# Moving a router into an attention loop: running ranks, scattered token numbers, expert weights split early

## The chip, the cores and the metric

The kernel runs on one core of a Trainium2 chip. The metric is the device time of one execution in microseconds (us). Engines are named as the profile names them: PE (matrix), PEld (its weight loads), DVE (vector), ACT (scalar), POOL (GpSimd), SP (the engine that issues most DMAs); "POOLq" or "SPq" is an engine's instruction queue.

## The reference

Two transformer layers on 16 x 256 tokens of width 256. Layer 0: layer norm, cross attention (16 heads of 16), residual; then a mixture of experts:

```
x = layernorm(x1)                                  # 4096 tokens
logits = x @ router_w + router_b                   # 16 experts
topv, topi = top_k(logits, 4); topw = softmax(topv)
gu = x @ gate_up[e] + bias;  act = (clip(up) + 1) * gate * sigmoid(1.702 * gate)
out = sum over the 4 chosen experts of topw * (act @ down[e] + down_bias[e])
```

Layer 1: layer norm and cross attention over batches at one position, residual, then a gated feed-forward with quantised weights, residual.

## The kernel before

Four parts run one after the other, each with an unrolled or looped schedule in which every engine has its own instruction list and semaphores order them. A part ends with a barrier, and `clear` (L44) sets an attention's semaphores to zero one by one on POOL.

**L0 attention** (`attention`, tag l0). 16 units of 256 tokens. `run_units` (L253) runs steps u = -5 to 16. In step u, with 16 sub-steps k (one a head), PE computes transposed scores of unit u (L554, into `ps_t`, two buffers), scores of unit u+2 (L567, into `ps_s`, two buffers) and the q, k, v projections of unit u+3; DVE takes the row maxima of `ps_s` (L453), ACT the exponentials of `ps_t` (L353). At k = 8 DVE makes the layer-norm statistics of unit u+4 (L439, L444), and POOL from them `rstd` (L331, L333), the normed tile `xn` (L337) and the residual with bias (L340); POOL also splits the context into high and low halves (L317, L319). DVE writes `v1` with its bias (L496) at k = 14, and the unit's output `yout` (L490) at k = 11 of the next step; SP stores it (L302). PE waits for the maximum of two slots before, and for the exponential of two slots before.

**Router** (`routed_experts`, first two blocks). Eight chunks of 512 tokens are loaded again from `x1`, normed, split into two f16 halves and stored as `moe_rows` (L762), transposed (L896) and multiplied with the router weights (L903); DVE adds the bias (L822), takes the eight largest (L827), their indices (L831). In the same loop the 16 experts' weights are loaded (L735, L736) and split: high half on ACT (L875, L876), low half on DVE (L857, L859). A second block computes on DVE ranks, first tiles and the row `pos` of each of the 16384 token-expert pairs (L944 to L978), and inverts that table into the token of each row by one-hot matmuls (L980 to L996, L1005, L1021). `slots` and `weights` go to memory in pieces of 16 bytes (L928, L929).

**Expert loop** (`cp_...`). 80 tiles of 256 rows. In step i POOL gathers the rows of tile i+3 with two indirect DMAs (L1109) by token numbers that DVE copied from SBUF (L1125); PE transposes tile i+1 (L1179), runs gate and up of tile i (24 matmuls, L1191) and down of tile i-2 (14 matmuls, L1200, L1202); DVE and ACT make the activation (L1131 to L1140, L1156, L1160), POOL its low half (L1114); ACT copies out y of tile i-2 (L1165) after `a_hi` of tile i, and SP stores it (L1091). All these orders are written out by hand.

**L1 attention** (L325 gathers eight times a unit what the experts wrote) and **gated_ffn** follow.

Of the kernel before, what the change touches and what calls it, by code (L numbers as in the profile page):

```python
# [7 lines left out]
ALU = mybir.AluOpType  # L8
# [9 lines left out]
P = 128  # L18
# [11 lines left out]
XB = 8  # L30
# [6 lines left out]
TILES = 80  # L37

# [24 lines left out]
def attention(nc, tag, x_in, x_out, ctx_t, w, masks, query_rows, key_rows, rows=None):  # L63
# [3 lines left out]
    with ExitStack() as ctx:  # L67
# [3 lines left out]
        adding = rows is not None  # L71
        K = 4
# [17 lines left out]
        w_raw = sb("w_raw", [P, 8, D])  # L90
# [6 lines left out]
        bv = sb("bv", [P, D])  # L97
# [3 lines left out]
        if masks:  # L101
            mraw = sb("mraw", [P, 2, QT, UNIT], I32)
# [15 lines left out]
        qs = sb("qs", [P, KQ, 8, UNIT], F16)  # L118
        ks = sb("ks", [P, KQ, H, UNIT], F16)
# [17 lines left out]
        yout = sb("yout", [P, 2, QT, D])  # L137

# [3 lines left out]
        w_high = sem("w_high")  # L142
# [3 lines left out]
        gp = sem("gp_setup")  # L146
        flagged = sem("flagged")
# [12 lines left out]
        with nc.Block() as block:  # L160
            @block.sync
            def _(sp):
# [9 lines left out]
                sp.dma_start(bv[:], w["bv"].partition_broadcast(P)).then_inc(const_loaded, 16)  # L172
# [6 lines left out]
                for i in range(2):  # L179
                    if masks:  # L180
                        sp.dma_start(mraw[:, i], masks[i]).then_inc(const_loaded, 16)
                sp.wait_ge(ks_set, 2)
                sp.dma_start(ks[96:rows_t].rearrange("p b h t -> p (b h t)"), key_rows).then_inc(rows_loaded, 16)
                if kinds:
                    sp.dma_start(qs[96:rows_s].rearrange("p b h t -> p (b h t)"), query_rows).then_inc(rows_loaded, 16)

# [7 lines left out]
            def _(pool):  # L194
                nc.gpsimd.memset(ident[:], 0.0).then_inc(gp, 1)
                nc.gpsimd.memset(ident16[:], 0.0).then_inc(gp, 1)
                nc.gpsimd.memset(half[:], -0.5).then_inc(gp, 1)
                pool.wait_ge(gp, 3)
# [4 lines left out]
                nc.gpsimd.memset(v1[:], 1.0).then_inc(gp, 1)  # L203

            @block.vector
            def _(dve):
                nc.vector.memset(ks[:, 0:2], 0.0).then_inc(ks_set, 1)
                for n, (src, dst, raw, by) in enumerate(weights):
                    dve.wait_ge(w_high, n + 1)
                    nc.vector.scalar_tensor_tensor(dst[:, 1], raw, by, dst[:, 0], ALU.mult, ALU.subtract)  # L210
                dve.wait_ge(const_loaded, 96 if masks else 64)
                dve.wait_ge(rows_loaded, 32 if kinds else 16)
                nc.vector.tensor_scalar(bq[:], bq[:], scale, None, ALU.mult)
                if masks:
# [10 lines left out]
                    nc.vector.tensor_copy(any_masked[:], count[:])  # L225

            @block.tensor
            def _(pe):
                if masks:
# [17 lines left out]
            "act": [xhi_done, qh_done, kh_done, mh_done, exp_done, osb_done, ahi_done],  # L247
            "dve": [stats_done, mv_done, xlo_done, ql_done, kl_done, v1_done, max_done, ml_done, rec_done, an_done, alo_done, y_done],
# [3 lines left out]

        def run_units(step):  # L253
            for u in range(-5, UNITS + 1):
                step(u)
# [386 lines left out]

# [958 lines left out]
```

## Time and profile before

| | |
|---|---|
| median of 3 runs | 1594.58 us (1590.15 to 1595.18) |
| profiled execution, its own time | 1595.34 us |
| its span, first to last instruction | 1593.5 us |
| granted TensorE clock, mean | 0.884 |
| busy: PE, DVE, POOL, ACT | 73%, 64%, 48%, 43% |
| L0 attention with its set-up, until its last store has landed | 0 to 421.5 us |
| router, until the first transposes of the expert loop | 421.5 to 600.9 us |
| expert loop | 600.9 to 996.2 us |
| L1 attention; feed-forward | 996.2 to 1410.7; 1410.7 to 1593.5 us |

A timeline row gives start, duration, engine, line, operation, output<-inputs, shape and count; the bracket is the engine's idle time before it and what ended it. For a DMA the duration is that of the issue, not of the transfer. In a table of windows each engine has its busy us and its instruction count.

### The profile page before, as it was taken

The numbers are of one execution on the slowest core, as the hardware profiler recorded it, in microseconds if no ns is written. First come the engines' busy times: TensorE is split into PE (matmuls) and PEld (weight loads), VectorE is DVE, ScalarE is ACT, GpSimd is POOL, SyncE is SP. The second block draws the span as 40 slices with busy tenths as digits, with TensorE's granted clock in tenths as the row PEclk, the third lists the DMA queues.
The fourth block names the chain that finished last, engine by engine and source line by source line (L and its number), as shares of the span: only waits on it lengthen the run. The fifth ranks groups of instructions, "written<-read, shape, count | busy, mean of one in ns | idle before, by whom it ended". The sixth has DMA issues, their size and how long they took to land. (4 is left out here: it accounts for less than half of the span.)

```text
span 1593.5 us, 35326 instructions
## 1 busy us (share of the span) xinstructions
PE 1168.3 (73%) x11045; PEld 890.5 (56%) x11047; DVE 1014.7 (64%) x2474; ACT 683.6 (43%) x1312; POOL 761.1 (48%) x783
## 2 busy tenths in 40 slices
PE   2688888888354248999999998026777777718997
PEld 1456666665153227888888887014666666504555
DVE  3777777775287995666666665137777776425563
ACT  1155555556253004555555554002444444524443
POOL 6332233310132376766666664488877772003443
PEclk9899999999755558999999999566999999958999
DMA  3212222210275412333333343544554452121231
GB/s 112 84 56 70 79 74 81 58 42 31 94 244 194 16 1 80 113 110 110 112 109 110 111 107 94 106 102 131 148 140 134 128 134 55 36 96 53 80 105 54
DMA packets 145101, 151.11 MB, mean 95 GB/s; under 512 B 32024, under 2 KB 131144, under 8 KB 144968
## 3 DMA queue, kind: packets, MB, share of 16 engines
q1 hardware_dynamic: 131168, 111.94, 24.3%
q0 software_dynamic: 13824, 37.77, 9.1%
q8 instruction: 63, 1.03, 0.3%
q14 instruction: 46, 0.38, 0.1%
HBM read 86.06 MB, written 37.88 MB: 78 GB/s over the span
## 5 line engine op out<-in xcount | busy, mean ns | idle before, releaser
L353 ACT ACTIVATE l_pt<-l_ps_t 128x512 f32<-128x512 f32 (+1 forms) x512 | 244.2, 493 | 296.7 <-PE l_ps_t L554 290.3
L453 DVE TENSOR_REDUCE l_mx<-l_ps_s 128x2 f32<-128x512 f32 (+1 forms) x512 | 274.3, 547 | 135.7 <-PE l_ps_s L567 135.3
L1191 PE MATMUL cp_ps_g<-cp_xt,ex_gu_hi 128*128 128x256 f16 x1280 | 216.6, 275 | 7.2 <-issue 4.4
L567 PE MATMUL l_ps_s<-l_ks,l_qs 96*128 96x256 f16 (+1 forms) x1024 | 172.3, 255 | 55.3 <-issue 35.7
L1109 POOL DMA_INDIRECT cp_rows<-moe_rows,cp_slot_token x160 | 169.1, 1057 | 45.0 <-issue 26.7
L1191 PE MATMUL cp_ps_g<-cp_xt,ex_gu_lo 128*128 128x256 f16 x640 | 175.6, 274 | 0.0
L554 PE MATMUL l_ps_t<-l_qs,l_ks 100*128 100x256 f16 (+1 forms) x1024 | 166.1, 248 | 4.6 <-ACT l_pt L353 3.9
L325 POOL DMA_INDIRECT l_picked<-expert_rows,l_slots x128 | 130.9, 1023 | 57.6 <-issue 37.0
L1131 DVE TENSOR_SCALAR cp_gate<-cp_ps_g,ex_g_bias 128x256 f32<-128x256 f32 x160 | 70.1, 479 | 123.1 <-PE cp_ps_g L1191 123.1
L1114 POOL TENSOR_TENSOR cp_a_lo<-cp_act_f,cp_a_hi 128x512 f16<-128x512 f32 x80 | 92.5, 1156 | 93.4 <-ACT cp_a_hi L1160 93.4
L1191 PEld LDWEIGHTS cp_ps_g<-cp_xt,ex_gu_hi 128*128 x1280 | 120.8, 98 | 26.7 <-issue 12.3
L567 PEld LDWEIGHTS l_ps_s<-l_ks,l_qs 96*128 96x128 f16 (+1 forms) x1024 | 89.0, 100 | 78.9 <-issue 51.4
L1151 ACT COPY cp_xt<-cp_ps_x 128x1024 f16<-128x1024 f16 x80 | 80.3, 1003 | 75.9 <-PE cp_ps_x L1179 75.9
L331 POOL TENSOR_SCALAR l_rstd<-l_mv 128x2 f32<-128x2 f32 x32 | 7.6, 238 | 217.5 <-DVE l_mv L444 217.3
L554 PEld LDWEIGHTS l_ps_t<-l_qs,l_ks 100*128 100x128 f16 (+1 forms) x1024 | 92.6, 99 | 31.2 <-ACT l_pt L353 13.9
L1160 ACT CAST cp_a_hi<-cp_act_f 128x512 f16<-128x512 f32 x80 | 49.4, 618 | 132.0 <-DVE cp_act_f L1140 132.0
L1376 POOL TENSOR_TENSOR ff_hlo<-ff_hf,ff_hhi 128x512 f16<-128x512 f32 x48 | 55.7, 1167 | 85.1 <-ACT ff_hhi L1405 85.1
L1202 PE MATMUL cp_ps_y<-ex_dn_hi,cp_a_hi 128*128 x320 | 87.5, 274 | 0.0
L1202 PE MATMUL cp_ps_y<-ex_dn_hi,cp_a_lo 128*128 x320 | 87.5, 273 | 0.0
L1202 PE MATMUL cp_ps_y<-ex_dn_lo,cp_a_hi 128*128 x320 | 87.5, 273 | 0.0
L337 POOL TENSOR_SCALAR l_xn<-l_xin,l_mv,l_rstd 128x256 f32<-128x256 f32 x64 | 77.8, 1223 | 3.4
L576 PE MATMUL l_ps_b<-l_ident,l_xn 128*128 128x128 f32 x128 | 22.6, 305 | 67.8 <-POOL l_xn L337 67.8
(228 smaller groups left out, 2912.4 us busy)
## 6 DMA issues: line engine op xcount, KB each, us to landing
expert_rows<-cp_yout SPq DMA_DIRECT2D x80, 256.0 KB
l_qs<-l_nat SPq DMA_DIRECT2D x96, 128.0 KB
l_ks<-l_nat SPq DMA_DIRECT2D x192, 64.0 KB, 2.6
l_cin<-in_ctxT SPq DMA_DIRECT2D x32, 256.0 KB, 2.9
x<-l_yout SPq DMA_DIRECT2D x64, 128.0 KB, 1.8
rt_raw<-in_gate_up SPq DMA_DIRECT2D x16, 512.0 KB, 4.3
l_xin<-in_x SPq DMA_DIRECT2D x32, 128.0 KB, 2.2
rt_xin<-x SPq DMA_DIRECT2D x8, 512.0 KB, 4.4
```

The costliest lines, as they stand in the source:

```text
L325: nc.gpsimd.indirect_dma_start(picked[:, n % 2, q, k], None, y_rows, bass.IndirectOffsetOnAxis(ap=slots[:, n * QT + q, k:k + 1], axis=0)). ...
L337: nc.gpsimd.tensor_scalar(xn[:, q], xin[:, n % XB, q], mv[:, q, 0:1], rstd[:, q:q + 1], ALU.subtract, ALU.mult).then_inc(xn_done, 1)
L353: nc.scalar.activation(pt[:, h % 8], ps_t[:, h % 2, :, 0:span], ACT.Exp).then_inc(exp_done, 1)
L453: nc.vector.reduce_max(mx[:, n % 2, :, 8 * (k % 2) + k // 2], ps_s[:, k % 2, :, 0:span], AX_X).then_inc(max_done, 1)
L554: last = nc.tensor.matmul(ps_t[:, h % 2, kt, 0:span], ks[0:rows_t, u % KQ, key_head, kt * P:kt * P + P], qs[0:rows_t, u % KQ, h // 2, seen ...
L567: last = nc.tensor.matmul(ps_s[:, h % 2, q, 0:span], qs[0:rows_s, n % KQ, h // 2, q * P:q * P + P], ks[0:rows_s, n % KQ, key_head, seen], ...
L1109: nc.gpsimd.indirect_dma_start(rows[:, n, h], None, rows_dram[:, :], bass.IndirectOffsetOnAxis(ap=slot_token[:, n, h:h + 1], axis=0)).then ...
L1114: nc.gpsimd.tensor_tensor(a_lo[:, b], act_f[:, b], a_hi[:, b], ALU.subtract).then_inc(alo_done, 1)
L1131: nc.vector.tensor_scalar(gate[:, b, m], ps_g[:, b, m], g_bias[:, bass.ds(e, 1), m], LIMIT * WS, ALU.add, ALU.min).then_inc(gate_done, 1)
L1151: nc.scalar.copy(xt[:, 1 - b], ps_x[:, 1 - b]).then_inc(xt_copied, 1)
L1191: last = nc.tensor.matmul(ps_g[:, b, m], wt[:, bass.ds(e, 1), c, m * P:m * P + P].rearrange("p o n -> p (o n)"), xt[:, b, part, c], start= ...
L1202: last = nc.tensor.matmul(ps_y[:, b, h], a[:, b, c, h * P:h * P + P], wt[:, bass.ds(e, 1), c].rearrange("p o n -> p (o n)"), start=False, ...
```

## The change

- `attention` for layer 0 gets a `route` object. The router's work is done there by units: in step u unit u-2's output is normed again (statistics from `yout` at k = 12 and 14 of the step before; four small POOL operations; two ACT activations at k = 3), split in halves (ACT at k = 5, POOL), stored, transposed by PE into a `ps_t` slot (k = 6), multiplied with the router weights into a `ps_s` slot (k = 12); DVE makes logits, maxima, indices and one-hot. In step u unit u-3 gets its ranks (PE, a `ps_s` slot at k = 4, against counts so far), positions (DVE), and POOL scatters its token numbers with eight indirect DMAs into `route.table`, a memory table with a fixed stretch of 4096 rows for each expert. The loop has two more steps (u = 17, 18).
- Expert weights 0 to 7 are loaded and split in steps -5 to 0 (`EXPERTS_AT`), 8 to 15 inside the first 16 tiles of the expert loop (`late_expert`), because `qs` and `ks` of the attention share SBUF with them. Weights of wq to wo and the mask are loaded into the experts' raw buffers. XB is 7 in layer 0.
- `v1` is written by ACT without bias; the bias goes through `wo` into `bo` in the set-up, in both layers.
- The router's two blocks are replaced by one short block (counts to tiles, first table row of each tile, weights, bias rows).
- In the expert loop the token numbers of a tile come by a DMA of SP from `route.table` at a row read from a register, instead of by a DVE copy; slots are computed in four DVE pieces in steps 1, 3, 5, 7 and stored by SP in step 9. The expert part ends with a `clear`.

The diff, cut to what the prediction speaks of:

```diff
@@ attention
+        XB = 7 if routing else 8
+                if routing:
+                    sp.dma_start(rw[:], route.rw); sp.dma_start(rb[:], ...)
+                    sp.wait_ge(zeroed, 1)
+                    sp.dma_start(route.table..., pt[...][:, 0:ROWS // P]).then_inc(table_set, 16)
                 sp.wait_ge(ks_set, 2)
                 sp.dma_start(ks[96:rows_t]..., key_rows)
+                dve.wait_ge(bv_done, 1)
+                nc.vector.scalar_tensor_tensor(bo[:], ps_b[:, 0], 1.0 / WS, bo[:], ALU.mult, ALU.add)
+        EXPERTS_AT = {-5: (0,), -4: (1, 2), -3: (3, 4), -2: (5,), -1: (6,), 0: (7,)} if routing else {}
+        ITERATIONS = range(-5, UNITS + (3 if routing else 1))
@@ sync, step u
+                def load_expert(e):
+                    if e >= 2:
+                        sp.wait_ge(e_low, 2 * (e - 1))
+                    route.load_expert(sp, e, e_loaded[e % 2])
+                    n = u - 2
+                        sp.dma_start(route.rows(n), xh[:, n % 2]...).then_inc(rows_stored[n % 2], 16)
+                    for e in EXPERTS_AT.get(u + 1, ()):
+                        load_expert(e)
+                    sp.wait_ge(scattered, 16 * QTILES * TOP)      # after the loop
@@ gpsimd, step u, in this order
+                    n = u - 2
+                        pool.wait_ge(mv2_done, c1 + 2 * n + 2)
+                        nc.gpsimd.tensor_scalar(rstd2[:], mv2[:, :, 1], EPS, None, ALU.add).then_inc(var2_done, 1)
+                        nc.gpsimd.tensor_scalar(shift2[:], mv2[:, :, 0], -1.0, None, ALU.mult).then_inc(minus_done, 1)
+                        nc.gpsimd.tensor_tensor(rstd2[:], rstd2[:], half[:], ALU.pow).then_inc(rstd2_done, 1)
+                        nc.gpsimd.tensor_tensor(shift2[:], shift2[:], rstd2[:], ALU.mult).then_inc(shift2_done, 1)
...
+                        pool.wait_ge(xhi2_done, c1 + n + 1)
+                        nc.gpsimd.tensor_tensor(xh[:, n % 2, :, 1], xn2[:], xh[:, n % 2, :, 0], ALU.subtract)
...
+                    n = u - 3
+                        pool.wait_ge(pos_done, c1 + n + 1)
+                        for q in range(QT):
+                            for k in range(TOP):
+                                nc.gpsimd.indirect_dma_start(route.table, bass.IndirectOffsetOnAxis(ap=route.pos[:, t, k:k + 1], axis=0),
+                                                             token_id[:, t:t + 1], None).then_inc(scattered, 16)
@@ scalar
+                    def norm_again(n):                            # k == 3, n = u - 2
+                        act.wait_ge(shift2_done, c1 + n + 1)
+                        for q in range(QT):
+                            nc.scalar.activation(xn2[:, q], yout[:, n % 2, q], ACT.Identity, bias=shift2[:, q:q + 1], scale=rstd2[:, q:q + 1])
+                    for e in EXPERTS_AT.get(u, ()):               # end of step u; DVE likewise with expert_low
+                        expert_high(e)
@@ routed_experts, first block
+                for e in (EARLY, EARLY + 1):
+                    route.load_expert(sp, e, e_loaded[e % 2])
+                sp.wait_ge(rows_zero, 1)
+                sp.wait_ge(bias_split, 2)
...
+                sp.wait_ge(weighed, 1)
+                sp.dma_start(weights_dram.rearrange("(t p) k -> p t k", p=P), wts[:]).then_inc(tables_stored, 16)
+                sp.wait_ge(bias_set, 32)
@@ expert loop, sync, step i
+                        if live(i, 3):
+                            if live(i, 1):
+                                sp.wait_ge(gathered[n], at_gather(i + 1, n))
+                            row = first_of(i + 3)
+                            sp.dma_start(row_token[:, n], route.table[bass.ds(row, R), :]...).then_inc(idx_loaded[n], 16)
                         if live(i, -2):
                             sp.wait_ge(y_copied, at(i - 2))
-                            sp.dma_start(y_dram[...].rearrange("(q p) d -> p q d", p=P), yout[:, b])
+                            sp.dma_start(y_dram[...].rearrange("(p h) d -> p h d", h=2), yout[:, b])
+                        if isinstance(i, int) and i == 9:
+                            sp.wait_ge(slot_step, 5)
+                            sp.dma_start(slots_dram..., slot[:]).then_inc(tables_stored, 16)
+                        e = late_expert(i)                        # 8 + i // 2 for even i < 16
+                        if e is not None and e + 2 < E:
+                            sp.wait_ge(e_low, 2 * (e - EARLY) + 2)
+                            route.load_expert(sp, e + 2, e_loaded[e % 2])
@@ gpsimd, step i
-                            pool.wait_ge(idx_set, at(i + 3))
+                            pool.wait_ge(idx_loaded[n], (i + 3 - n) * 8 + 16)
@@ vector and scalar, end of step i
+                            act.wait_ge(e_loaded[e % 2], 32 * ((e - EARLY) // 2 + 1))
+                            for part, raw in zip((0, 2), route.raw_parts(e)):
+                                nc.scalar.activation(route.part(e, part), raw, ACT.Copy, scale=WS).then_inc(e_high, 1)
+                            dve.wait_ge(e_high, 2 * (e - EARLY) + 2)
+                            for part, raw in zip((1, 3), route.raw_parts(e)):
+                                nc.vector.scalar_tensor_tensor(route.part(e, part), raw, WS, route.part(e, part - 1), ALU.mult, ALU.subtract)
@@ tensor, before gate and up of tile i
+                            if isinstance(i, int) and EARLY <= i < E:
+                                pe.wait_ge(e_low, 2 * (i - EARLY) + 2)
@@ class Route
+    def load_expert(self, sp, e, loaded):
+        sp.dma_start(self.raw[:, e % 2, 0:KC], self.gate_up[e * D:e * D + D, :]...).then_inc(loaded, 16)
+        sp.dma_start(self.raw[:, e % 2, KC]..., self.down[e * D:e * D + D, :]...).then_inc(loaded, 16)
```

## Rows read from the trace of the kernel before

**Rows 1.** Windows: router, expert loop; busy us (x instructions) by engine, clock, DMA.

```profile
421.50:600.88 179.38, 67.26 (x321) 53.43 (x323) 143.69 (x479) 40.69 (x50) 78.11 (x110) 0.50 0.47 120
600.88:996.20 395.32, 380.34 (x3680) 332.05 (x3680) 250.32 (x558) 213.22 (x321) 258.20 (x237) 0.98 0.35 106
```

**Rows 2.** Waits of SP at the end of L0: total us, times, longest.

```profile
SPq L46 <- PEq L46: 4.2, 1, 4.2
SPq L306 <- DMA x<-l_yout: 3.1, 1, 3.1
```

**Rows 3.** Windows: one unit of the L0 loop in its steady part.

```profile
222.03:243.93 21.90, 19.44 (x196) 13.86 (x195) 16.51 (x35) 12.51 (x25) 6.42 (x8) 1.00 0.24 74
```

**Rows 4.** Timeline of POOL: rstd of units 0, 5 and 15 in L0.

```profile
22.00 0.23 POOL L331 TENSOR_SCALAR l_rstd<-l_mv 128x2 f32<-128x2 f32 x1
...
111.75 0.23 POOL L331 TENSOR_SCALAR l_rstd<-l_mv 128x2 f32<-128x2 f32 x1 [14.63 <-DVE l_mv L444]
...
332.67 0.23 POOL L331 TENSOR_SCALAR l_rstd<-l_mv 128x2 f32<-128x2 f32 x1 [13.27 <-DVE l_mv L444]
```

**Rows 5.** Groups of the router stage: count, busy us, mean ns, idle before.

```profile
L903 PE MATMUL rt_ps_l<-rt_rw,rt_xt 128*128 128x16 f32 x128 | 28.7, 375 | 9.3 <-ACT rt_xt L882 9.3
...
L875 ACT ACTIVATE ex_gu_hi<-rt_raw 128x1024 f32 x12 | 12.6, 1054 | 5.4 <-DMA rt_raw<-in_down 5.4
L876 ACT ACTIVATE ex_dn_hi<-rt_raw 128x512 f32 x12 | 7.4, 618 | 0.0
...
L857 DVE SCALAR_TENSOR_TENSOR ex_gu_lo<-rt_raw,ex_gu_hi 128x1024 f32 x12 | 14.5, 1210 | 0.0
L859 DVE SCALAR_TENSOR_TENSOR ex_dn_lo<-rt_raw,ex_dn_hi 128x512 f32 x12 | 8.1, 677 | 0.0
```

**Rows 6.** Timeline of DVE across a step's end in L0.

```profile
229.75 0.74 DVE L496 SCALAR_TENSOR_TENSOR l_v<-l_ps_b,l_bv 128x256 f32<-128x256 f32 x2
...
233.51 0.69 DVE L453 TENSOR_REDUCE l_mx<-l_ps_s 128x2 f32<-128x512 f32 x1 [0.18 <-PE l_ps_s L567]
```

**Rows 7.** Timeline of POOL: residual after xn; an indirect gather in L1.

```profile
225.69 1.26 POOL L340 TENSOR_TENSOR l_xin<-l_xin,l_bo 128x512 f32<-128x512 f32 x1
...
1185.12 0.95 POOL L325 DMA_INDIRECT l_picked<-expert_rows,l_slots  x1 [0.30 <-issue]
```

**Rows 8.** DMA issues: count, KB each, median us to landing.

```profile
rt_raw<-in_gate_up SPq DMA_DIRECT2D x16, 512.0 KB, 4.3
rt_raw<-in_down SPq DMA_DIRECT2D x16, 256.0 KB, 5.3
slots<-ex_pos SPq DMA_DIRECT2D x1, 64.0 KB, 12.1
weights<-ex_wts SPq DMA_DIRECT2D x1, 64.0 KB, 19.0
rt_rw<-in_router_w SPq DMA_DIRECT2D x1, 16.0 KB, 1.8
```

**Rows 9.** Timeline of one tile of the expert loop.

```profile
640.52 0.59 ACT L1165 ACTIVATE cp_yout<-cp_ps_y 128x512 f32<-128x512 f32 x1
...
641.18 0.27 PE L1200 MATMUL cp_ps_y<-ex_bias_rows,ex_two_rows 128*128 x1
641.35 14.47 SPq L1091 DMA_DIRECT2D expert_rows<-cp_yout  x4
...
642.08 0.97 POOL L1109 DMA_INDIRECT cp_rows<-moe_rows,cp_slot_token  x1
...
647.47 0.61 PE L1179 MATMUL cp_ps_x<-ex_ident,cp_rows 128*128 128x128 f16 x8
```

**Rows 10.** Waits in 640 to 980 us.

```profile
PEld cp_ps_x L1179 <- DMA cp_rows<-moe_rows,cp_slot_token: 2.2, 6, 0.4
```

**Rows 11.** Timeline: a DVE copy beside a POOL operation in the router.

```profile
472.07 2.12 POOL L799 TENSOR_TENSOR rt_xh<-rt_xn,rt_xh 128x1024 f16<-128x1024 f32 x1 [2.57 <-ACT rt_xh L880]
...
472.36 1.87 DVE L832 COPY rt_best<-rt_high 128x16 f32 x1
```

More of the change, by code:

```diff
@@ new lines, in step @@
+                        if routing and k == 4 and live(n):
+                            at = s_at["rank", n]
+                            pe.wait_ge(max_done, c1 + at - 1)
+                            pe.wait_ge(took_done, c1 + n + 1)
+                            for q in range(QT):
+                                earlier = [(route.ones[:], took[:, n % 2, a]) for a in range(1 + q)] + [(before[:], took[:, n % 2, 1 + q])]
+                                for i, (l, r) in enumerate(earlier):
+                                    last = nc.tensor.matmul(ps_s[:, at % 2, 0, q * E:q * E + E], l, r, start=i == 0, stop=i == len(earlier) - 1)
+                            last.then_inc(s_done, 1)
@@ new lines, in step @@
+                        n = u - 2
+                        if routing and k == 12 and live(n):
+                            at = s_at["logits", n]
+                            pe.wait_ge(max_done, c1 + at - 1)
+                            pe.wait_ge(exp_done, c1 + t_at["turn", n] + 1)
+                            for q in range(QT):
+                                for c in range(KC):
+                                    last = nc.tensor.matmul(ps_s[:, at % 2, 0, q * E:q * E + E], xt2[:, c, q * P:q * P + P], rw[:, c], start=c == 0, stop=c == KC - 1)
+                            last.then_inc(s_done, 1)
@@ new lines, in routed_experts @@
+        fills = sb("fills", [P, E]); one_e = sb("one_e", [P, E]); tile_id = sb("tile_id", [P, 1]); tile_row = sb("tile_row", [P, 1])
+        over = sb("over", [P, E, E]); tiles = sb("tiles", [P, E]); end = sb("end", [P, E]); jump = sb("jump", [P, E])
+        past = sb("past", [P, E - 1]); jumped = sb("jumped", [P, E - 1]); owner = sb("owner", [P, 1]); base = sb("base", [P, 1])
+        expert = sb("expert", [1, TILES], U32); first_row = sb("first_row", [1, TILES], U32)
+        region = sb("region", [P, E - 1]); posf = sb("posf", [P, T * K]); slot = sb("slot", [P, T, K], U32)
@@ L1081, in expert_of, with first_of, late_expert @@
                 return nc.values_load(expert[0:1, bass.ds(i, 1)], engines=[engine], min_val=0, max_val=E - 1,
-                                      skip_runtime_bounds_check_because="the minimum with E - 1 bounds it")
+                                      skip_runtime_bounds_check_because="it counts ends of 15 experts")
+            def first_of(i):
+                return nc.values_load(first_row[0:1, bass.ds(i, 1)], engines=[mybir.EngineType.SP], min_val=0, max_val=ROWS - R,
+                                      skip_runtime_bounds_check_because="a tile past an expert's end is of the next expert, and the last region holds every tile")
+            def late_expert(i):
+                return EARLY + i // 2 if isinstance(i, int) and i % 2 == 0 and 0 <= i // 2 < LATE else None
             with nc.Block() as block:
```

808 lines of the change are left out of this document (427 added, 381 removed).

## The prediction

> **What bounds the kernel now.** I read first the table of windows by stage [rows 1]. From the last landing of L0 [rows 2] to the first transposes of the expert loop there are 179.4 us in which PE works 67 at half clock and DVE 144: the stage that the change removes. In the expert loop PE is busy 380 of 395 us: that stage is PE's, unless something starves it. Then one unit of L0 [rows 3]: 21.9 us, PE busy 19.4, DVE 16.5, ACT 12.5, POOL only 6.4. PE bounds it, with DVE close by, and POOL is nearly free. The steps follow each other at (332.67 - 111.75) / 10 = 22.1 us [rows 4]. Last the waits and the timeline of the expert loop [rows 9, 10]: PE waits on gathered rows 6 times in 340 us, 2.2 us in all. So the gathers arrive just in time. The change makes the gathers later, and this is why the loop needs a working of its own.
>
> **The removed stage.** After: barrier and clear as before, 4.2 + 0.6 us for 58 semaphores [rows 2]; the 32 more at the same rate add 2.5. Then the short block. The DVE chain with two PE transposes is some 25 small operations, about 8 us; POOL's bias-row memset ends at about 6 us. SP sends the bias rows at 7 and the softmax weights at 9.5. The block does not wait for the latter, but they are 4096 pieces of 16 bytes; the like table took 12.1 us to land, and its twin behind it on the queue 19.0 [rows 8]. The first token-number load sits behind them on SP's queue, and lands at 21.8 us instead of 16. Two gathers (2.8 us) and their landing (1.9) follow: 26.5 us after the block's start. 4.8 + 2.5 + 26.5 = 33.8; gain 179.4 - 33.8 = **-145.6** (-138 to -151: the table stored slower, or not in the way).
>
> **L0, set-up: +3** (+1 to +4). Three more DMAs (0.4 us of issue each) and a table of zeros ahead of the key rows, whose landing opens DVE's last stretch; `bo` gets one more operation. L1's set-up gets the latter.
>
> **L0, filling: +16** (+8 to +20). Expert 0 is loaded in about 5 us [rows 8], split by ACT in 1.05 + 0.62 and by DVE in 1.21 + 0.68 [rows 5]. All that stands ahead of unit 0's statistics on DVE, which end at 22 us now [rows 4] and then at about 32.6: 10 us beyond the set-up's. Expert 2 can be loaded only when expert 0 is split, so ACT and DVE reach unit 0's transposed tile at 38 and 40: no more lost, as `xn` comes then too. Experts 3 and 4 end 2.5 us after the first scores, 5, 6 and 7 cost about 1.2 each at a step's end, since `v1` leaves DVE.
>
> **L0, steady steps: +33** (+22 to +50). Per unit PE gets 4 transposes (0.6 us, as L604 has them), the logits: 28.7 us for 4096 tokens at half clock [rows 5], so 0.9 a unit at full clock, and 5 small rank products (0.4): 1.9. DVE gets 3.4 us (two statistics 0.74, the rest fifteen operations of 0.07 to 0.3) less 0.74 for `v1`. Part of it falls at k = 12 to 0, where DVE has no gap now [rows 6]; at k = 4 to 7 it has some. That makes 25 us a step. POOL has a chain of its own. After the statistics at k = 8 it makes `xn` and the residual, 4.9 us (222.0 to 226.95 [rows 3, 7]); then eight scatters. No scatter is in the trace; the nearest row is a gather of 128 rows, 0.95 + 0.30 [rows 7], so 10.3 with the slower ones. I take it, since the instruction makes 128 descriptors either way; half (small elements) and double are the ends. Then the four small operations for the next norm, 1.8, on which ACT waits at k = 3 before further exponentials, and PE behind it at k = 6; from there to the statistics it is 8.2. Sum 25.2. Both chains are about equal: 25.4. Steps 3 to 11 (those with scatter and statistics): 9 x 3.3 = 30; step 2: 3. With scatters at half the step is PE's 24.5, +22 in all. Steps 12 to 15: **+10** (+6 to +14), 2.5 each, PE's 1.9 and a hop.
>
> **L0, tail: +29** (+20 to +38). The last unit now ends with a store that lands 3.8 us after `yout`. After: statistics, four POOL operations, norm, halves: POOL is free at about 8 us for the scatters of unit 14 (10.3), then of unit 15 (10.3), landing 1.9: 30.4. So +26.6, and 2 for the work between.
>
> **The skill, beside the trace.** A DVE copy of 16 columns took 1.87 us beside a POOL operation that ended at the same moment [rows 11]. The Trainium skill (SBUF — State Buffer, SBUF: two separate sides) says that a VectorE operation with two SBUF inputs, or in a two-port mode, and a GpSimd operation lock each other out of a shared port for the whole instruction; the trace agrees. By that rule the added one-hot and rank product would lose up to 1 us a step beside POOL's 15 us of work; the sum would be about 10 us higher. I have not added it.
>
> **Expert loop, tiles 18 to 79: +27** (+5 to +60). Call T the end of gate and up of tile i. One tile before the rows shown T is 636.5 (641.2 less a period of 4.7). `yout` of tile i-2 ends at 641.1 [rows 9], T + 4.6, and its store is issued at T + 4.85. Before, the gather of tile i+4 starts at 642.08, T + 5.6, and PE takes its rows at 647.47, T + 11, with some 0.9 us to spare. After, SP issues the token-number load only behind that store: T + 5.4, plus a register read that the trace doesn't show (0.1 to 1; I take 0.3, as SP's other waits cost little). The smallest landing is 1.8 [rows 8], but it follows a store of 256 KB: 2.2. So the gather starts at T + 7.9, 2.3 later; less the spare 0.9, 1.4 us late over three tiles, 0.46 a tile, x 59 = 27. If the load lands at 1.6 the loss is 15; if 4 us, +60. POOL's `a_lo` behind the gather is still in time.
>
> **Tiles 0 to 17: +38** (+20 to +55). In even steps to 10 SP waits, after the store, until DVE has split an expert. ACT starts its halves after `yout`, T + 4.6, ends at 6.3; DVE ends at 8.2, having waited 3 us. SP then issues the next expert, 768 KB (5 us to land [rows 8]), and behind it lies the next token-number load: T + 13.5; gather and landing T + 18, and that tile's gate and up end at T + 21.1. With one such tile in each pair, twice the pair less 4.7 is 21.1: a pair takes 12.9 instead of 9.5. In the first four pairs the slot pieces (2 us each, at one element a cycle) bring it to 13.8. 4 x 4.3 + 2 x 3.4 + 2 x 1.5 = 27; PE's wait for expert 15 at tile 15, 4; the slot table of step 9 (12.1 us to land) in front of a token-number load, 7.
>
> **The rest: 0.** Clear after the experts 2.5, barrier and L1 set-up 1.5: +4. In L1 `v1` leaves DVE, which has no gap there: -4.
>
> **Sum.** 3 + 16 + 33 + 10 + 29 = 91 in L0; -145.6; +38 + 27; +4 - 4: +10. On the profiled 1595.3 that is 1606; the median of the runs is 0.8 lower: **1605**.
>
> **Rivals.**
> 1. *Token numbers cost nothing* (faster). The load lands before POOL is done with its `a_lo`, or its lateness fits in the spare 0.9 us. For it: the spare, and small DMAs in 1.8 us [rows 8, 9]. Against: the load waits behind a store that itself waits for `yout`. It decides when issue to landing is under about 1.1 us, or when SP's store goes out 1.4 us earlier. Then -27 in the loop and about -7 in the head, whose delays are then only the expert loads': 1571. Chance 0.33, which also takes in an L0 that hides more than I think (its low end alone gives 1575).
> 2. *POOL's chain binds L0*: a scatter costs more than a gather, or ACT's wait at k = 3 isn't absorbed at all: 2.4 us more a step and 5 in the tail, 1632. For it: POOL goes from 6 to 20 us a step. Against: eight gathers a unit fit in L1. Chance 0.14.
> 3. *Token numbers come very late*: 4 us from issue to landing, because stores, gathers and this load share the DMA engines: +33, 1638. Chance 0.13.
> 4. *The forecast*: all chains as worked out, 1585 to 1625: chance 0.40.
>
> **How the numbers follow.** A measurement of this kernel tells about 0.3% (4.8 us) from no change. Faster by more: rival 1, and 0.05 of the forecast case: 0.38. Same: 0.11, slower: 0.51, from the rest of the forecast case and rivals 2 and 3. The range reaches from 1550 (rival 1 with part of L0's low ends) to 1650 (rival 3 with some of the high ones). The forecast case's own is 1585 to 1625.
>
> **What would show it.** In the profile after: unit 0's `rstd` near 33 us; L0 steps 25 us apart, with POOL busy about 19 of them, and ACT waiting on `shift2`; the last scatter about 30 us after the last `yout`; the first cp transposes about 34 us after it has landed; gaps before cp transposes that end on gathered rows, and POOL waiting on the token-number load; tiles 5.2 us apart instead of 4.7, 6 to 7 in the first sixteen. I'm wrong if the tiles stay at 4.7 (then it is faster), or if L0's steps go beyond 27.

## The result, and the profile after

The changed kernel takes 1676.83 us (median of four executions; three lie between 1668.76 and 1679.48, and the fourth, 6287 us and unlike any other, counts in this median, which would be 1674.17 without it, and not in the ratio). The kernel before took 1594.88 on the same chip. The ratio is 1.051 (95% interval 1.048 to 1.054): 5% slower, where 0.7% was forecast, and outside the range of 1550 to 1650.

The profiled execution spans 1677.7 us against 1593.5. Cut at the same events, with the prediction's terms beside:

| stretch | before | after | change | predicted |
|---|---|---|---|---|
| start to `rstd` of unit 5 (set-up, filling) | 111.8 | 130.5 | +18.7 | +19 |
| to `rstd` of unit 15 (ten steady steps) | 220.9 | 252.1 | +31.2 | +33 |
| to the last `yout` (steps 12 to 15) | 84.2 | 97.5 | +13.3 | +10 |
| to the first transposes of the expert loop (tail, router) | 184.0 | 69.3 | -114.7 | -116.6 |
| to `a_lo` of tile 18 | 97.4 | 153.0 | +55.7 | +38 |
| to `a_lo` of tile 79 | 291.1 | 365.5 | +74.4 | +27 |
| to the end (clear, L1, feed-forward) | 604.2 | 609.9 | +5.7 | 0 |

Five of the seven come out within 6 us. The expert loop does not: 65 of the 74 us by which the sum is short are there.

POOL's timeline in L0, `rstd` of units 0, 5 and 15 (compare [rows 4]):

```profile
30.23 1.11 POOL L459 TENSOR_SCALAR l_rstd<-l_mv 128x2 f32<-128x2 f32 x1 [6.15 <-DVE l_mv L685]
...
130.47 0.23 POOL L459 TENSOR_SCALAR l_rstd<-l_mv 128x2 f32<-128x2 f32 x1 [17.18 <-DVE l_mv L685]
...
382.59 0.23 POOL L459 TENSOR_SCALAR l_rstd<-l_mv 128x2 f32<-128x2 f32 x1 [5.41 <-DVE l_mv L685]
```

Unit 0's is at 30 us (33 was said). The idle time ahead of unit 15's ends on DVE's `mv` and not on POOL's own work. In every step from unit 5 to unit 15 POOL sits idle for 4.1 us or more ahead of `rstd`. That alone does not tell whether its chain binds, since the chain of the prediction has such a wait in it (8.2 us, from the four small operations to the statistics); e4 below tells.

The tail, timeline of all engines from the last `yout` to the next block:

```profile
480.12 0.69 DVE L754 SCALAR_TENSOR_TENSOR l_yout<-l_ps_a,l_xin 128x512 f32<-128x512 f32 x1 [2.83 <-PE l_ps_a L775]
...
490.94 1.07 POOL L475 DMA_INDIRECT row_tokens<-l_token_id,ro_pos  x1 [0.17 <-issue]
...
512.86 0.95 POOL L475 DMA_INDIRECT row_tokens<-l_token_id,ro_pos  x1 [0.30 <-issue]
524.06 0.35 POOL L989 MEMSET ex_ident<- 128x128 f32 x2 [10.25 <-POOLq L53]
```

A scatter costs 0.95 + 0.30 us, as the gather did [rows 7]. The last one ends 33 us behind `yout`; landing, barrier and clear take 10.3, the short block 25.3 to the first transposes at 549.38.

The two halves of the expert loop as windows:

```profile
549.40:702.40 153.00, 107.53 (x884) 88.51 (x885) 85.72 (x135) 63.22 (x92) 64.03 (x60) 0.82 0.38 96
702.40:1076.90 374.50, 306.85 (x2798) 245.89 (x2796) 189.72 (x366) 162.03 (x246) 187.05 (x179) 0.99 0.29 86
```

PE was busy 96% of the loop [rows 1]; now 70% of its first part and 82% of its second. A tile takes 365.5 / 61 = 5.99 us instead of 4.77. What PE, its weight loads and POOL wait for is in the waits of 700 to 1060 us (total us, times, longest), beside [rows 10]; the last line is the landing of the token-number loads in 700 to 1040 us:

```profile
PE cp_ps_x L1255 <- DMA cp_rows<-moe_rows,cp_row_token: 41.7, 33, 4.2
PEld cp_ps_x L1255 <- DMA cp_rows<-moe_rows,cp_row_token: 26.6, 20, 2.6
POOL cp_rows L1162 <- PE cp_ps_x L1255: 101.5, 42, 3.7
POOL cp_rows L1162 <- DMA cp_row_token<-row_tokens: 41.2, 15, 3.6
DMA to landing us min/median/max: 1.7/2.1/4.3
```

The view puts 42 of POOL's waits down to PE, but they too are waits for the token numbers. The transposes that the gather needs are those of two tiles before and were done 4 to 8 us earlier, while the first gather of a tile starts 0.85 us behind the landing of its load in every one of 54 tiles (24 to 77), whichever of the two the view names.

One lap of the chain, in the timeline of 808 to 818 us: the store that SP issues when `yout` is copied, the token-number load behind it, the two gathers, the transposes that take their rows.

```profile
808.49 0.34 SPq L1136 DMA_DIRECT2D expert_rows<-cp_yout  x1
...
809.54 0.34 SPq L1132 DMA_DIRECT2D cp_row_token<-row_tokens  x1
...
812.27 0.96 POOL L1162 DMA_INDIRECT cp_rows<-moe_rows,cp_row_token  x1 [2.65 <-DMA cp_row_token<-row_tokens]
...
813.54 0.94 POOL L1162 DMA_INDIRECT cp_rows<-moe_rows,cp_row_token  x1 [0.30 <-issue]
...
817.50 0.29 PE L1255 MATMUL cp_ps_x<-ex_ident,cp_rows 128*128 128x128 f16 x2 [1.61 <-DMA cp_rows<-moe_rows,cp_row_token]
```

Gate and up of the first of these tiles ended at 803.73, so the store is at T + 4.8, as predicted. Over the 55 tiles between 705 and 1035 us the load is issued 1.33 us behind the store on average (1.04 to 1.81), and the first gather starts 3.1 us behind the load (2.5 to 5.1). The prediction had 0.85 and 2.2.

### The profile page after: what moved, and what is told of

It reads as the page before. It is cut to its first block and busy times, and to the rows that moved or that the text cites. A ratio compares the mean times of both kernels' runs of the same rounds, so it can differ in the third digit from the quotient of the medians.

```text
span 1677.7 us, 35011 instructions
## 1 busy us (share of the span) xinstructions
PE 1182.5 (70%) x11011; PEld 875.6 (52%) x11012; DVE 944.4 (56%) x2206; ACT 710.4 (42%) x1391; POOL 854.1 (51%) x904
## 5 line engine op out<-in xcount | busy, mean ns | idle before, releaser
L1162 POOL DMA_INDIRECT cp_rows<-moe_rows,cp_row_token x160 | 161.1, 1007 | 251.9 <-DMA cp_row_token<-row_tokens 112.7
L1270 PE MATMUL cp_ps_g<-cp_xt,ro_wexp 128*128 128x256 f16 x1920 | 241.4, 286 | 25.9 <-issue 15.5
L1270 PEld LDWEIGHTS cp_ps_g<-cp_xt,ro_wexp 128*128 x1920 | 191.0, 103 | 65.3 <-issue 35.9
L475 POOL DMA_INDIRECT row_tokens<-l_token_id,ro_pos x128 | 125.1, 977 | 40.6 <-issue 39.5
L858 PE MATMUL l_ps_s<-ro_wexp 96*128 96x256 f16 x512 | 103.5, 287 | 34.5 <-issue 17.1
L1255 PE MATMUL cp_ps_x<-ex_ident,cp_rows 128*128 128x128 f16 x640 | 51.8, 227 | 96.0 <-DMA cp_rows<-moe_rows,cp_row_token 95.7
L1282 PE MATMUL cp_ps_y<-ro_wexp,cp_a_hi 128*128 x640 | 115.0, 274 | 0.0
L825 PE MATMUL l_ps_t<-ro_wexp 100*128 100x256 f16 x512 | 100.2, 279 | 1.6 <-ACT l_pt L490 0.8
L858 PE MATMUL l_ps_s<-l_ks,l_qs 104*128 104x128 f16 x512 | 72.7, 231 | 34.8 <-issue 24.0
L1282 PE MATMUL cp_ps_y<-ro_wexp,cp_a_lo 128*128 x320 | 87.2, 273 | 0.0
## 6 DMA issues: line engine op xcount, KB each, us to landing
x<-l_yout SPq DMA_DIRECT2D x64, 128.0 KB
ro_wexp<-l_nat SPq DMA_DIRECT2D x48, 128.0 KB
l_qs<-l_nat SPq DMA_DIRECT2D x48, 128.0 KB
```

The lines of the kernel that those rows point to most:

```text
L475: nc.gpsimd.indirect_dma_start(route.table, bass.IndirectOffsetOnAxis(ap=route.pos[:, t, k:k + 1], axis=0), token_id[:, t:t + 1], None).th ...
L825: last = nc.tensor.matmul(ps_t[:, at % 2, kt, 0:span], ks[0:rows_t, u % KQ, key_head, kt * P:kt * P + P], qs[0:rows_t, u % KQ, h // 2, see ...
L858: last = nc.tensor.matmul(ps_s[:, at % 2, q, 0:span], qs[0:rows_s, n % KQ, h // 2, q * P:q * P + P], ks[0:rows_s, n % KQ, key_head, seen], ...
L1162: nc.gpsimd.indirect_dma_start(rows[:, n, h], None, route.rows_dram[:, :], bass.IndirectOffsetOnAxis(ap=row_token[:, n, h:h + 1], axis=0)) ...
L1255: last = nc.tensor.transpose(ps_x[:, n, part, c, h * P:h * P + P], rows[:, n, h, part * D + c * P:part * D + c * P + P], ident16[:])
L1270: last = nc.tensor.matmul(ps_g[:, b, m], route.wexp[:, bass.ds(e, 1), cols:cols + P].rearrange("p o n -> p (o n)"), xt[:, b, part, c], sta ...
```

## The experiments

All times are medians; the ratio is to the kernel before on the same chip, with its 95% interval. The table has the us between the same events as above, each from one profiled execution; those of e6 and e13 were 10 and 12 us above their medians. e4 gathers row 0 in most tiles, so its last two columns are not to be compared; e11 is the kernel before with one edit.

| kernel | median | ratio | to unit 5 | to unit 15 | to last `yout` | to first transposes | tiles 0-17 | tiles 18-79 |
|---|---|---|---|---|---|---|---|---|
| changed | 1676.8 | 1.051 | 130.5 | 252.1 | 97.5 | 69.3 | 153.0 | 365.5 |
| e1 | 1597.2 | 0.999 | 128.0 | 260.2 | 99.7 | 72.2 | 132.8 | 295.5 |
| e2 | 1668.5 | 1.043 | 129.9 | 258.8 | 99.4 | 71.6 | 151.1 | 351.3 |
| e3 | 1658.9 | 1.039 | 130.3 | 256.6 | 99.0 | 70.9 | 130.6 | 364.3 |
| e4 | 1673.3 | 1.046 | 131.0 | 249.7 | 90.2 | 51.0 | 157.1 | 394.6 |
| e5 | 1580.9 | 0.992 | 128.2 | 253.0 | 97.1 | 69.5 | 130.8 | 294.9 |
| e6 | 1583.8 | 0.992 | 130.1 | 259.0 | 98.8 | 68.3 | 132.2 | 295.1 |
| e7 | 1593.9 | 1.001 | 119.1 | 278.8 | 97.6 | 69.4 | 129.1 | 294.3 |
| e8 | 1598.6 | 1.003 | 128.7 | 257.4 | 98.2 | 68.6 | 147.5 | 296.2 |
| e9 | 1567.5 | 0.984 | 125.4 | 261.9 | 101.2 | 62.1 | 122.6 | 294.2 |
| e10 | 1665.4 | 1.045 | 129.2 | 257.6 | 98.5 | 61.8 | 146.1 | 365.7 |
| e11 | 1593.3 | 1.000 | 111.2 | 221.1 | 84.9 | 185.5 | 95.9 | 290.7 |
| e12 | 1566.1 | 0.984 | 128.7 | 251.1 | 100.6 | 61.9 | 124.8 | 294.8 |
| e13 | 1569.0 | 0.984 | 129.3 | 264.6 | 98.7 | 61.3 | 122.2 | 294.7 |

**e1: the token numbers ahead of the store.**

```diff
-                        if live(i, 3):
...
-                                sp.wait_ge(gathered[n], at_gather(i + 1, n))
-                            row = first_of(i + 3)
+                        if live(i, 4):
...
+                                sp.wait_ge(gathered[b], at_gather(i + 2, b))
+                            row = first_of(i + 4)
...
```

> Only SP's order in the expert loop is changed: in each of its steps it asks for the token numbers of tile i+4 ahead of the store of tile i-2, where the changed kernel asks for those of tile i+3 and so sits behind the store of the step before. Theory (the token numbers stand behind a store that waits for yout, and a chain of three tiles runs through store, load, gather and transposes): tiles 18 to 79 go from 5.99 us back to about 4.77, which is 74 us, and the first eighteen tiles get back 15 to 30 of their 56, since every token number has one tile more of slack: 1570 to 1590 us, below the kernel before. Rival A (the loads and gathers are slow by themselves, 2.9 and 3.1 us, since they share the DMA engines with the stores): the order does not matter, gain under 15 us, 1660 or more. Rival B (the register that the address comes from holds SP up, wherever it stands): gain of about half, 1635.

1597.23 us, 0.999 (0.996 to 1.002): the edit is worth some 80 us, and the kernel is level with the one before, 7 us above the forecast's upper end. Tiles 18 to 79 take 4.84 us each, 295.5 in all; the first eighteen got 20 back. SP's timeline, and PE's wait for rows in 706 to 960 us, which was 27.6 us in 20 times:

```profile
800.48 0.34 SPq L1131 DMA_DIRECT2D cp_row_token<-row_tokens  x1
804.24 0.34 SPq L1135 DMA_DIRECT2D expert_rows<-cp_yout  x1
805.82 0.34 SPq L1131 DMA_DIRECT2D cp_row_token<-row_tokens  x1
```

```profile
PE cp_ps_x L1255 <- DMA cp_rows<-moe_rows,cp_row_token: 0.8, 1, 0.8
```

The load at 805.82 still follows a store, but it is for a tile further on. Rival A falls: a gather still takes 2.9 us to land (median; 3.1 in the changed kernel), and PE does not wait for it. So does rival B: the register is still read ahead of every load, and the gain is not halved.

**e8: the same, by taking the store off SP's queue.** ACT issues the store of `yout` behind its own copy; SP's order stays.

> The changed kernel with one edit: ACT issues the store of yout itself, right behind the copy, and SP's queue holds the token-number loads in the order that they had. Theory (it is the place behind the store that makes the token numbers late, not the number of steps that they are asked for ahead): the same as e1_load_first, tiles 18 to 79 at 4.8 to 4.9 us, 1595 to 1605 us; ACT gains 0.4 us a tile and has room for it (2.7 of 6 us busy). Rival (what helped in e1 was the tile more of lead, which this kernel does not give): 5.5 us a tile or more, 1640.

1598.62 us, 1.003 (1.001 to 1.005), tiles at 4.86 us. So it is the place behind the store. The first eighteen tiles gained only 5.5 us, where e1 gained 20: there the lead of one tile matters too. I read that as the wait for DVE's halves, which in e8 still stands right ahead of the next token numbers; this was not tried by itself.

**e2: no register read.** `row = first_of(i + 3)` and its address replaced by the constant `route.table[0:R, :]`; every tile gathers the same rows.

> The address of each token-number load is a constant instead of a register read from SBUF, so each tile gathers the rows of the first 128 entries (this leaves out that each tile has its own rows); the order stays. Between the issue of a store and that of the next token-number load the changed kernel shows 1.05 to 1.59 us. Theory (the read is a link of the chain over three tiles): the gap falls to 0.4 us, the chain gets 0.7 to 1.2 us shorter, 0.3 a tile, 15 to 25 us in all: 1652 to 1662 us. Rival (the read goes on while SP waits for yout, the gap is the store's own): no change beyond 5 us, 1677.

1668.47 us, 1.043 (1.038 to 1.048). SP's timeline:

```profile
803.37 0.34 SPq L1134 DMA_DIRECT2D expert_rows<-cp_yout  x1
803.87 0.32 SPq L1130 DMA_DIRECT2D cp_row_token<-row_tokens  x1
809.35 0.34 SPq L1134 DMA_DIRECT2D expert_rows<-cp_yout  x1
810.09 0.32 SPq L1130 DMA_DIRECT2D cp_row_token<-row_tokens  x1
```

The gap is 0.50 or 0.74 us instead of 1.04 or 1.56: the read costs 0.7 us (the prediction had 0.3). The Trainium skill (DMA: Bandwidth & Descriptors, Latency and other measured facts) gives a register load a floor of some 600 ns; the 0.7 us agree with it. Tiles 18 to 79 take 14.2 us less, 0.23 each, just short of the 15 to 25 expected, and the median is 6 to 8 us lower (without and with the outlier of the changed kernel). That 0.23 is a third of 0.7 is chance, though: issued so soon behind the store, the load takes 2.6 us to land (mean) instead of 2.3, so that the gather starts only 0.36 us earlier behind the store; another 0.24 come from its rows being there sooner. Together that is a lap of three tiles 0.6 us shorter.

**e3: no late experts.** `late_expert` returns None, tiles of experts 8 to 15 use expert 7's weights.

> The late experts 8 to 15 are neither loaded nor split (tiles of theirs take expert 7's weights, which leaves that part of the computation out); the order of SP's queue stays. Theory (in the even steps SP waits for DVE's halves and then puts 768 KB ahead of the next token numbers): tiles 0 to 17 lose 56 us now and would keep only what the queue order costs, 18 x 1.2 = 22, and some us for the slot pieces, so about 30 us less: 1647 us. Rival (the first tiles are slow because of the clock and the slot pieces): under 10 us, 1668 or more. Tiles 18 to 79 should not change in either.

1658.91 us, 1.039 (1.034 to 1.044), 15 to 18 us below the changed kernel where 30 were expected: 22 us in tiles 0 to 17, nothing behind them. But with the late experts gone one tile still took 17.2 us, the one behind the store of the slot table.

**e4: a quarter of the scatters.** `for k in range(TOP)` in POOL's step becomes `range(1)`.

> Of the four scatters of each 128 tokens only the first is done (the others' entries of the table stay at zero, so those tiles gather row 0), 2 a unit instead of 8. Theory (POOL's chain and the chain of PE and DVE are about equal in L0's steps, and the tail waits for two sets of scatters): tail 15 us shorter, steps 0.5 to 1 us shorter, 6 to 11 us: 1650 to 1657 us. Rival A (POOL's chain alone sets the steps): 2 us or more a step, 1632. Rival B (the steps don't see POOL at all): the tail alone, 1662.

1673.26 us, 1.046 (1.040 to 1.051). The steady steps took 249.7 us (251 to 265 in the kernels with eight scatters and the experts at the same steps), the last four 90.2 instead of 97.5, the tail 51.0 instead of 69.3: the first transposes came 27.5 us earlier. With 7.5 us less of scatters on POOL the steady steps hardly changed, so POOL's chain does not set them; the last four got 7 us shorter, so there the scatters count. The time hardly moved because the loop, in which most tiles now gather row 0, took 33 us more; that side effect was not foreseen.

**e5, e13: the late expert's load.** SP's wait for DVE's halves and the load of the next expert move one step on, behind the store: `e = late_expert(i - 1)`. e5 is e1 with this edit, e13 is e9 (below) without it.

> The kernel of e1_load_first (token numbers asked for ahead of the store), and SP issues the next late expert one step later, in the odd steps behind the store, when DVE's halves have long been done. Theory (in tiles 0 to 17 the wait for the halves, which end 8.2 us after gate and up, holds back SP's store and token numbers of the step after): the wait goes, a pair of tiles takes 10.5 us instead of the 12 to 13 of e1, tiles 0 to 17 shrink from 120 to about 105 us: 1582 us. Rival (the 768 KB on the queue and the work of DVE and ACT on the halves set the pair): under 5 us, 1593 or more; and since the expert then comes later, PE may wait for it, which would cost up to 10.

> e9_whole_rows with SP's late expert load back in the even steps, where it waits for DVE's halves. The median of e5_expert_next was 16 us below that of e1_load_first, but their profiles show the same 120 us for tiles 0 to 17. Theory (that edit does nothing, and the difference lay in parts that both kernels share): within 5 us of e9, 1567. Rival (it takes waits away that the profiled executions happened not to show): 1580.

e5 took 1580.85 us, 0.992 (0.990 to 0.994). The forecast of 1582 was met by luck, not by the theory: in the profiled executions tiles 0 to 17 took 130.8 us against 132.8, and 12 of the 18 us between the two spans stand ahead of the loop, where both kernels are the same. e13 says the same of the kernel with the other tables: 1569.03 against e9's 1567.46, and 122.2 us against 122.6. Once the token numbers have a tile of lead, this wait costs 2 us at most in these tiles. Why the medians of e1 and e5 lie 16 us apart, with no overlap of their executions (but on two chips), stays open. The prediction's account of tiles 0 to 17 put most of its 38 us on it.

**e6, e9, e10, e11: the tables in pieces of 16 bytes.** e6 is e5 with both tables stored from ACT's queue. e9 is e5 with the tables in the order of the partitions:

```diff
-        v = a.rearrange("(b g n) k -> n b g k", b=16, n=8)
+        v = a.rearrange("(p t) k -> p (t k)", p=P).rearrange("(g n) (b h k) -> n b h g k", n=8, b=16, h=2)
...
-                sp.dma_start(weights_dram.rearrange("(t p) k -> p t k", p=P), wts[:])
+                sp.dma_start(weights_dram.rearrange("(p t) k -> p t k", p=P), wts[:])
```

e10 is this edit alone on the changed kernel, e11 on the kernel before.

> As e5_expert_next, and the two tables of 4096 pieces of 16 bytes (weights ahead of the loop, slots at step 9) are stored from ACT's queue instead of SP's. Theory (the pieces block what is behind them on the same queue, 10.8 us and 13.6 us to landing): 5 us less ahead of the first transposes and 5 to 8 less around tile 9: 10 to 13 us below e5. Rival (the pieces fill the DMA engines for every queue): under 3 us.

> As e5_expert_next, and the two tables lie in DRAM in the order of the partitions, so that a store is 128 pieces of 512 bytes instead of 4096 of 16; L1 reads them in pieces of 16 bytes as before. Theory (the 16-byte pieces hold up every DMA, on whatever queue: e6_tables_act moved them to ACT's queue and tile 11 came 15.2 us behind tile 10 all the same, 17.7 in e5): the long tile goes, 11 to 13 us less, and 4 to 5 us less ahead of the first transposes: 1562 to 1567 us. Rival (the long tile has another cause, as the order of SP's queue at step 9): within 4 us of e5, 1581.

> The changed kernel with nothing but the tables in the order of the partitions. Theory (terms of the prediction: 5.8 us ahead of the first token number and 7 us at step 9; the traces have 17 us for that tile in place of about 6): 13 to 18 us less, 1659 to 1664 us. Rival (in the queue's order of the changed kernel the token numbers are late anyway, and hide it): under 6 us, 1671 or more.

> The kernel before with the tables in the order of the partitions. Theory (there the tables are stored behind the last step of the router and the loop's first gathers wait 10.5 us for rows, while the table pieces are under way): 5 to 9 us less, 1587 us. Rival (the gathers wait for their own chain and not for the pieces): no change, 1595.

e6 took 1583.82 us, 0.992 (0.989 to 0.995), the same as e5: its rival held. The Trainium skill (DMA: Bandwidth & Descriptors, Issuing engines are not separate DMA queues) says that transfers started by different engines run on the same 16 DMA engines and interleave; the rows agree. Landing of the tables in the changed kernel, then in e9 (KB, us):

```profile
weights<-ex_wts SPq DMA_DIRECT2D x1, 64.0 KB, 10.8
slots<-ex_slot SPq DMA_DIRECT2D x1, 64.0 KB, 13.6
```

```profile
weights<-ex_wts SPq DMA_DIRECT2D x1, 64.0 KB, 1.8
slots<-ex_slot SPq DMA_DIRECT2D x1, 64.0 KB, 3.8
```

And the 16 us from 620 us on in e5, then in e9, where the slots were stored at 615.7 and at 619.4 (windows; the last three numbers are clock, DMA share, GB/s):

```profile
620.00:636.00 16.00, 7.29 (x50) 5.63 (x50) 4.84 (x9) 3.85 (x6) 1.80 (x2) 0.68 0.91 147
```

```profile
620.00:636.00 16.00, 12.87 (x121) 10.51 (x118) 9.21 (x16) 9.46 (x15) 9.34 (x9) 1.00 0.62 200
```

With 16-byte pieces the DMA engines are 91% busy and move less; PE works 7.3 us instead of 12.9, and its granted clock is 0.68 instead of 1.00. e9 took 1567.46 us, 0.984 (0.980 to 0.988): 8 us less than e5 in tiles 0 to 17 and 7 ahead of the first transposes. With e1's edit and this one the change is 1.6% faster than the kernel before, with e5's edit (e9) or without it (e13). e10 took 1665.42, 1.045 (1.041 to 1.050), 9 to 11 us below the changed kernel, 7.5 + 6.9 us in the same two stretches: a little short of the 13 to 18 expected, far from the rival. e11 took 1593.34, 1.000 (0.998 to 1.002), as its rival had it: in the kernel before the tables cost nothing. Only the change put other work behind them.

**e7: early experts spread.** `EXPERTS_AT = {-5: (0,), -3: (1,), -1: (2,), 2: (3,), 4: (4,), 6: (5,), 8: (6,), 10: (7,)}`, on e6.

> As e6_tables_act, and the eight early experts are split in steps -5, -3, -1, 2, 4, 6, 8 and 10 of L0 instead of -5 to 0. Theory (in the filling steps the eight splits cost 16 us, mostly expert 0's 10 ahead of unit 0's statistics and what ACT and DVE do at a step's end; in the steady steps PE and DVE have next to no gap, so a split costs 1.9 to 2.5 us there as well): within 4 us of e6, either way. Rival (steady steps hide a split, since DVE is busy 18.6 of 24.9 us there): 8 us faster.

1593.85 us, 1.001 (0.998 to 1.003), 10 us slower than e6: dearer than both theories had. The filling gets 11 us back, but the ten steady steps take 278.8 us against 259.0, some 4 for each of the five splits moved into them, at a granted clock of 0.92.

**e12: DVE's low halves one step later**, on e9: `e = late_expert(i - 1) if isinstance(i, int) and i < 14 else late_expert(i)` in DVE's step, slot pieces in the steps between.

> As e9_whole_rows, and DVE makes the low halves of a late expert one step after ACT has made the high ones (expert 15 as before), with the slot pieces in the even steps between. Theory (tiles 0 to 17 still take 111 us against 85 in the kernel before, because DVE waits 2.6 us for ACT at the end of each even step, and the next tile's gate stands behind it; eight such waits are 20.7 us): a pair takes 10 us instead of 12.6, 14 to 18 us less: 1550 to 1554 us. Rival (the halves' own work, 1.8 us of DVE and 1.6 of ACT, and the landing of the expert set the pair, since a buffer is free only when DVE is done): under 5 us, 1563 or more; an expert that lands later could even cost some us.

1566.13 us, 0.984 (0.980 to 0.987), no gain. The first ten tiles did shrink (pairs of 10.8 us instead of 12.6), and tiles 11 to 15 gave it back. DVE's wait for ACT is a part of those pairs, but e9's first eighteen tiles take 25 us more than those of the kernel before, and more of that is in PE's waits (551 to 673 us of e9):

```profile
PE cp_ps_g L1270 <- ACT cp_xt L1222: 9.1, 7, 2.9
PE cp_ps_x L1255 <- DMA cp_rows<-moe_rows,cp_row_token: 8.3, 8, 2.4
PE cp_ps_g L1270 <- DVE ro_wexp L1211: 6.2, 1, 6.2
```

The wait for rows is no longer than in the kernel before (10.5 us, at the loop's start). 9.1 us are waits for ACT's copy of the transposed rows, which ACT makes behind the late expert's high halves (1.56 us). 6.2 us are one wait, of tile 15 for DVE's halves of expert 15; e12 leaves it as it was (6.2), and the changed kernel has it too (6.6). No run took these two away by themselves.

## Why the prediction was wrong

**The step that failed** is the term "Expert loop, tiles 18 to 79: +27 (+5 to +60)", and in it the line "So the gather starts at T + 7.9". Its mechanism was right: store at T + 4.8, load behind it, a loss shared by three tiles; e1 and e8 show it. The links were mis-sized. This is one lap, from a store to the store three tiles on, as the prediction has it and as the mean of 53 laps of the changed kernel's timeline:

| link | predicted | measured |
|---|---|---|
| store to issue of the load (register read) | 0.85 | 1.32 |
| issue of the load to its landing | 2.2 | 2.26 |
| landing to the first gather | 0 | 0.85 |
| first gather to the transposes | 4.5 | 5.03 |
| transposes to the end of gate and up (T) | 3.1 | 3.73 |
| T to the next store | 4.85 | 4.83 |
| lap | 15.5 | 18.02 |

18.02 over three is the 6.0 us of a tile. The landing was priced well. The largest miss is the time between the landing and the gather that waits for it, which the prediction put at nothing without a reason; no row of the trace before shows such a pair. The register read, "(0.1 to 1; I take 0.3, as SP's other waits cost little)", measured 0.7. With these two the gather starts 1.4 us later than forecast, 2.8 us too late instead of 1.4: 0.93 us a tile, x 59 = 55 in the prediction's own formula. The rest of the 74 is in the two links behind it, which the prediction took from a loop in which PE hardly waits; why they are longer was not tried.

Rival 3 (token numbers very late) is not what happened: it wanted 4 us from issue to landing, and the mean was 2.3, with 4.3 at most. Even its price, +60 in this term, is below the 74.

The error in judgement was to add up a chain that is repeated sixty times from the links that the trace names, and to price the others at nothing or by hope. Each us on that chain is worth 20 in the sum.

**Tiles 0 to 17: +38, measured +56**, at the upper bound of 55, and for other reasons than told. e1, e10 and e3 account for some 50 of it, if their gains add up: the queue order 20 (not seen as a part of its own), the slot table 7 (7 predicted), the late experts 22 (27 + 4), where e5 and e13 show that SP's wait for the halves has no share in it once the numbers have a lead. What the late experts cost there is, by PE's waits in e9, mostly ACT's high halves ahead of its copy for PE (9.1 us) and the wait for expert 15 (6.6 in the changed kernel; the prediction had 4).

**The removed stage and the tail: right.** -114.7 against -116.6; the 16-byte table behind which the first token numbers stood was worth 7.5 us (e10; 5.8 predicted), and the tail's two sets of scatters cost what a gather costs.

**L0: right in sum** (+63.2 against +62). The filling, +16, holds, and e7 shows that the steady steps would have been the dearer place. The steady step was forecast at 25.4 us with PE's and POOL's chains about equal. The rows show 24.7 us for most steps, and e4 speaks against rival 2 (POOL's chain binds). What brings the mean to 25.2 are single long steps (below), which no step of the prediction had, so that +31 against +33 is in part luck. In steps 12 to 15 (+13.3 against +10) the prediction had PE's work alone, and by e4 the scatters have 7 us of it.

**The end: +5.7 against 0.** Clear and start of L1 +2.1. L1 took 3.6 us more, where 4 less were forecast for `v1` on ACT; between the profiled executions L1's length differs by as much (411.3 in e5, 414.8 in e1), so the sign stays open.

**Rival 1** (token numbers cost nothing, 1571) is near what the change becomes when the numbers have their lead: 1597 in e1, 1581 in e5. That e9 comes to 1567 is no proof of its sum, since e9 has the tables in rows as well, which rival 1 had not. Its aside that L0's low end alone gives 1575 is a slip: the low ends add up to 57 instead of 91, which is 1571.

## What to carry to other kernels

Before a value that another engine waits for is fetched by a new DMA, look at what is ahead of it on the issuing queue, above all a store that waits for the end of a tile: ask for the value one tile further ahead, or issue the store elsewhere. Price a chain that is repeated link by link, also the links that no row names: here 0.85 us from a landing to the start of the gather that waits for it, and 0.7 us for a register read. A table written in 16-byte pieces is free where nothing stands behind it and costs a tile or two where something does (7 us in each of two places here); write it in the order of the partitions.

## What the runs showed of the hardware

- 64 KB in 4096 pieces of 16 bytes took 10.8 and 13.6 us to land and in 128 pieces of 512 bytes 1.8 and 3.8; from ACT's queue it was 10.5 and 12.8, and held up SP's queue all the same: behind the slots one issue of SP took 8.3 us in e5, and in e6 three took 1.5 to 2.5, where the others take 0.35.
- An indirect gather on POOL that waited for its token numbers started 0.85 us behind their landing (0.85 or 0.86 in 54 of 54 tiles of the changed kernel). PE's transposes started 0.12 us behind the landing of their rows (median). What fills the 0.85 isn't shown.
- A scatter of 128 numbers of four bytes took POOL 0.95 us and 0.30 to the next, as a gather of 128 rows of 1 KB did.
- In e4, where most tiles gather row 0 over and over, the gathers took 3.8 us to land (median) instead of 3.1, and the loop 33 us more. In the changed kernel the rows differ. Why one row for all is slower isn't shown.
- L0's steps in the new kernels take 24.7 us, but of the ten steady ones one to four in an execution took 26 to 36 (41 in e7). The kernel before has none. Here are windows of one step of 24.7 us, of the long one behind it, and of three times 4 us in the long one (the last three numbers are clock, DMA share, GB/s):

```profile
203.95:228.64 24.69, 21.06 (x213) 15.29 (x212) 18.66 (x51) 14.64 (x30) 16.77 (x21) 1.00 0.47 75
228.64:257.37 28.73, 22.48 (x213) 15.73 (x212) 18.49 (x51) 14.74 (x30) 16.74 (x20) 0.94 0.46 68
232.00:236.00 4.00, 3.52 (x39) 2.44 (x39) 3.49 (x10) 1.34 (x3) 3.44 (x4) 1.00 0.22 68
236.00:240.00 4.00, 1.64 (x15) 1.25 (x13) 2.07 (x10) 2.07 (x4) 3.01 (x4) 1.00 0.97 147
240.00:244.00 4.00, 2.40 (x22) 1.54 (x26) 1.99 (x5) 1.07 (x2) 3.12 (x4) 0.82 1.01 93
```

  The DMA engines are full for 8 us, PE stands still for 4 of them ahead of the scores, and then the granted clock falls from 1.00 to 0.82. Of these 8 us (236 to 244) the DMA view has, by queue, packets, MB and share of the 16 engines:

```profile
q1 hardware_dynamic: 1041, 0.96, 98.0%
q0 software_dynamic: 96, 0.00, 1.1%
```

  So it is the loads and stores of SP's queue that fill the engines, and not the scatters, which are the small packets of the other. e4, with a quarter of the scatters, has such steps too. Between profiled executions of the same code up to there, the first transposes came at 547.7 to 560.1 us. That may be why e5 looked faster than e1; it is not shown. Which of SP's transfers it is, and why they take longer in such a step, wasn't tried.
